# Layer 0 of a two-layer transformer: queries and gates of a head by seven half-size products, key blocks through memory, residual input loaded late

## The reference

```
qkv = silu(x @ qkv_w.T)                 # per head: q, k, v of 128
for blk in blocks:                      # per head
    scores = (q @ k.T) * diag_decay
    out = scores @ v + (q * q_decay) @ kv
    kv = kv * block_decay + (k * k_decay).T @ v
attn = out * rsqrt(mean(out**2) + eps) * norm_w
gate = sigmoid(x @ gate_w.T)
y = (gate * attn) @ out_w.T
x = layernorm(x + y)
```

## Time and profile before

| | |
|---|---|
| median of 3 runs | 3100.72 us |
| profiled execution, own time | 3099.54 us |
| its span | 3097.8 us |
| PE busy | 2976.4 us, 96% |
| DVE, ACT, POOL busy | 63%, 48%, 51% |
| mean granted clock of PE | 0.986 of full speed |
| end of layer 0's attention | about 1160 us |

### The profile page before, as it was taken

One profiled execution on the slowest core, in us unless ns is written; L12 is line 12 of the kernel. 1 busy time (PEld: TensorE's weight loads), 2 busy tenths in 40 slices (PEclk: granted clock), 3 DMA queues, 4 the chain that ended last, 5 costly groups with the idle time before them and its releaser, 6 DMA issues. The chain is left out here.

```text
span 3097.8 us, 56941 instructions
## 1 busy us (share of the span) xinstructions
PE 2976.4 (96%) x17632; PEld 2666.8 (86%) x17632; DVE 1946.6 (63%) x3061; ACT 1490.4 (48%) x2887; POOL 1574.9 (51%) x1075
## 2 busy tenths in 40 slices
PE   7999999999999987799999999999999999996998
PEld 7999999999999976799898998989998989885886
DVE  3445454454545456577777777777777777775565
ACT  3333333333333322466666666666666666663221
POOL 3333333333333331366666666566666666654664
PEclk9999999999999998899999999999999999998999
DMA  4211221121211110366666666656666666655541
GB/s 126 60 51 57 59 61 51 52 62 56 59 51 54 56 28 25 100 206 196 204 205 193 205 196 203 209 189 205 204 199 201 197 202 206 196 195 180 152 142 48
DMA packets 311499, 413.83 MB, mean 134 GB/s; under 512 B 35968, under 2 KB 242832, under 8 KB 311312
## 3 DMA queue, kind: packets, MB, share of 16 engines
q1 hardware_dynamic: 273728, 278.05, 31.2%
q10 hardware_dynamic: 37680, 135.02, 11.0%
q0 software_dynamic: 32, 0.02, 0.0%
HBM read 259.85 MB, written 136.31 MB: 128 GB/s over the span
## 5 line engine op out<-in xcount | busy, mean ns | idle before, releaser
L1365 ACT ACTIVATE b_prob<-b_s_ps,b_shift 128x1024 f32<-128x1024 f32 x256 | 285.8, 1117 | 347.5 <-DVE b_shift L1515 339.8
L82 PE MATMUL b_pj_kq<-b_w_hi,xT_hi 128*128 128x384 f32 x1008 | 351.7, 349 | 21.6 <-DVE b_nat L1491 20.1
L506 ACT ACTIVATE a_sig<-a_pj 128x512 f32<-128x512 f32 x192 | 114.8, 598 | 486.6 <-PE a_pj L84 486.5
L83 PE MATMUL b_pj_kq<-b_w_lo,xT_hi 128*128 128x384 f32 x1008 | 342.7, 340 | 0.0
L84 PE MATMUL b_pj_kq<-b_w_hi,xT_lo 128*128 128x384 f32 x1008 | 342.6, 340 | 0.0
L1521 DVE STREAM_TRANSPOSE b_blocks<-b_prob 128x1024 f32<-128x1024 f32 x256 | 317.4, 1240 | 25.5 <-ACT b_prob L1365 24.9
L1287 POOL TENSOR_TENSOR b_pT_lo<-b_pT_lo,b_pT_hi 128x1024 fp32r<-128x1024 f32 x128 | 305.0, 2405 | 14.4 <-ACT b_pT_hi L1354 14.3
L1287 POOL TENSOR_TENSOR pT_lo<-pT_lo,pT_hi 128x1024 fp32r<-128x1024 f32 x128 | 305.0, 2405 | 14.1 <-ACT pT_hi L1354 14.1
L1515 DVE TENSOR_REDUCE b_shift<-b_s_ps 128x1 f32<-128x1024 f32 x256 | 307.1, 1200 | 2.4 <-PE b_s_ps L84 2.4
L82 PE MATMUL a_pj<-b_w_hi,xT_hi 128*128 128x256 f32 x1024 | 295.6, 289 | 11.9 <-DVE xT_lo L647 11.3
L401 POOL TENSOR_TENSOR b_w_lo<-b_w_raw,b_w_hi 128x512 fp32r<-128x512 f32 x96 | 123.7, 1289 | 332.3 <-ACT b_w_hi L457 325.4
(11 more groups left out here) (257 smaller groups left out, 8907.3 us busy)
## 6 DMA issues: line engine op xcount, KB each, us to landing
bounce<-b_blocks ACTq DMA_DIRECT2D x256, 512.0 KB, 3.4
pT_lo<-bounce SPq DMA_DIRECT2D x512, 128.0 KB, 3.1
b_pT_lo<-bounce SPq DMA_DIRECT2D x512, 128.0 KB, 2.8
b_w_raw<-in_w SPq DMA_DIRECT2D x32, 768.0 KB, 5.0
b_w_raw<-in_w SPq DMA_DIRECT2D x95, 256.0 KB, 3.2
a_k_raw<-a_k_blocks SPq DMA_DIRECT2D x512, 32.0 KB, 1.8
a_w_raw<-in_w SPq DMA_DIRECT2D x32, 256.0 KB, 2.7
a_ow_raw<-in_ow SPq DMA_DIRECT2D x32, 256.0 KB, 3.1
```

The costliest lines, as they stand in the source:

```text
L82: pe.matmul(out, w_hi, x_hi, start=first, stop=False)
L83: pe.matmul(out, w_hi, x_lo, start=False, stop=False)
L506: act.activation(out, pj[half][:, :], ACT.Sigmoid).then_inc(sig, 1)
L1365: act.activation(prob[t % 2][:, :], s_ps[t % 2][:, :], ACT.Exp, bias=shift[:, t:t + 1], accum_out=row_sum[:, t:t + 1]).then_inc(exp_done, 1)
```

## The change

Call the gate and query weights of a head the rows of a 2x2 block matrix, with the lower and upper 256 features as its columns: a11, a12 (gate) and a21, a22 (query). The tokens are b11, b12 (lower features, first and second 512 tokens) and b21, b22 (upper). The four results are the gates and queries of either half of the tokens. Before, they take eight products of half the features; now they take seven, P1 to P7, in the form of Strassen's method with fewer additions:

The diff, cut to its core:

```diff
 def move_k(g):
     sp.wait_ge(k_blocked, g + 1)
+    sp.dma_start(k_bounce[...], k_blocks[...]).then_inc(k_moved, 16)
+    sp.wait_ge(k_moved, MOVED * g + 16)
     for c in range(GROUPS):
-        for r in range(GROUPS):
-            sp.dma_start(k_raw[c * BLK:(c + 1) * BLK, r]..., k_blocks[r * BLK:(r + 1) * BLK, c]...)
+        sp.dma_start(k_raw[c * BLK:(c + 1) * BLK]..., k_bounce[:, :, c, :]...)
...
+def weight_sums(g):                                   # POOL, slot 0
+    pool.wait_ge(w_in[Q_W], 32 * (g + 1))
+    wait(pool, proj, NP * g)
+    pool.tensor_tensor(to[S1], raw(a21), raw(a22), ALU.add).then_inc(w_summed, 1)
+    pool.tensor_tensor(to[S3], raw(a11), raw(a21), ALU.subtract).then_inc(w_summed, 1)
+    pool.wait_ge(w_summed, 4 * g + S1)
+    pool.tensor_tensor(to[S2], to[S1], raw(a11), ALU.subtract).then_inc(w_summed, 1)
+    pool.wait_ge(w_summed, 4 * g + S2)
+    pool.tensor_tensor(to[S4], raw(a12), to[S2], ALU.subtract).then_inc(w_summed, 1)
...
+def product(g, p):                                    # PE
+    if p == P1: pe.wait_ge(silu, 6 * g + 3)
+    if p == P6: wait(pe, combined, NC * (g - 1) + C21)
+    if p == P5: wait(pe, combined, NC * (g - 1) + C12)
+    if p == P2: pe.wait_ge(kept, g + 1)
+    if p == P7: pe.wait_ge(combined, NC * g + U2)
+    if p == P4: pe.wait_ge(combined, NC * g + U3)
+    if p == P3: pe.wait_ge(combined, NC * g + C22)
...
+    for k in range(2):
+        last = three_pass(pe, out[:, :], weights[0][:, k, :], weights[1][:, k, :], tokens[0][:, k, :],
+                          tokens[1][:, k, :], first and k == 0, k == 1, True)
...
+def combine(g, bg, n):                                # DVE
+    dve.wait_ge(proj, NP * g + {U2: P6, U3: P7, C22: P5, C21: P4, C12: P3}[n])
+    dve.tensor_tensor(to, onto, c_ps[n in (C22, C12)][:, :], ALU.add).then_inc(combined, 1)
...
-for h in range(2):                                    # SP, start
-    for t in range(4):
-        if h or t not in (K_W, V_W):
-            load_weights(h, t)
+load_weights(0, Q_W)
+load_weights(0, GATE_W)
+sp.dma_start(norm_sb[:, :], norm_w).then_inc(const_in, 16)
 load_decays(0, 0)
-sp.dma_start(sh.x_nat[:, :, :], x.rearrange("(t p) d -> p t d", p=P)).then_inc(x_nat_in, 16)
+for t in range(4):
+    load_weights(1, t)
...
+sp.wait_ge(proj, NP * HEADS)                          # SP, end
+sp.dma_start(sh.x_nat[:, :, :], x.rearrange("(t p) d -> p t d", p=P)).then_inc(const_in, 16)
```

More of the change, by code:

```diff
@@ L252, in l0_attention @@
         state = sb("state", [P, NT, HD])
+        state_flat = state[:, :, :].rearrange("p c d -> p (c d)")
         gated = sb("gated", [P, TOK])
@@ L410, in half_out, with token_sums_low @@
+            def token_sums_low():
+                for n in (2, 3):
+                    pool.wait_ge(x_hi_done, 2 * KB + n + 1)
+                    pool.tensor_tensor(t_lo[n], t_raw[n], f(t_hi[n]), ALU.subtract).then_inc(t_split, 1)
+                pool.wait_ge(x_summed, 2 * KB)
+                pool.memset(sq_sum[:, :], 0.0).then_inc(zeroed, 1)
+                pool.wait_ge(zeroed, 6)
             def half_out(h, b, j):
@@ L496, in sigmoid, with token_sums_high @@
+            def token_sums_high(*which):
+                for n in which:
+                    act.wait_ge(x_summed, 2 * n + 2)
+                    act.activation(t_hi[n], t_raw[n], ACT.Copy).then_inc(x_hi_done, 1)
             def sigmoid(g, bg, s):
-                act.wait_ge(proj, NG * g + s + 1)
+                act.wait_ge(proj, NP * g + s + 1)
                 half = s % 2
-                if s >= GATE.start:
-                    wait(act, gated_done, 2 * (g - 1))
-                    out = gate_T[bg][:, half * HALF:(half + 1) * HALF]
-                else:
-                    wait(act, silu, 6 * g + s - 1 if s >= 2 else 6 * (g - 1) + 5 + s)
-                    out = sig_tmp[half][:, :]
@@ L506, in sigmoid, with keep_first, gate_sigmoid @@
-                act.activation(out, pj[half][:, :], ACT.Sigmoid).then_inc(sig, 1)
+                wait(act, silu, 6 * g + s - 1 if s >= 2 else 6 * (g - 1) + 6 - s)
+                act.activation(sig_tmp[half][:, :], pj[half][:, :], ACT.Sigmoid).then_inc(sig, 1)
+            def keep_first(g, bg):
+                act.wait_ge(proj, NP * g + P1)
+                wait(act, attn, 2 * (g - 1))
+                act.activation(q_T[bg][:, 0:HALF], pj[0][:, :], ACT.Copy).then_inc(kept, 1)
+            def gate_sigmoid(g, bg, half):
+                cut = slice(half * HALF, (half + 1) * HALF)
+                wait(act, gated_done, 2 * (g - 1))
+                if half == 0:
+                    act.wait_ge(proj, NP * g + P2)
+                    act.activation(gate_T[bg][:, cut], pj[0][:, :], ACT.Sigmoid).then_inc(sig, 1)
+                else:
+                    act.wait_ge(combined, NC * g + C12)
+                    act.activation(gate_T[bg][:, cut], gate_T[bg][:, cut], ACT.Sigmoid).then_inc(sig, 1)
@@ L508, in step, with query_sigmoid @@
+            def query_sigmoid(g, bg, half):
+                act.wait_ge(combined, NC * g + (C21, C22)[half])
+                wait(act, silu, 6 * g + 3 + half)
+                act.activation(sig_tmp[half][:, :], q_T[bg][:, half * HALF:(half + 1) * HALF],
+                               ACT.Sigmoid).then_inc(sig, 1)
             def step(h, b, attention, project, output, split):
@@ new lines, in project_group, with weights_of @@
+                for u in range(2):
+                    cut = slice((2 * s + u) * P, (2 * s + u + 1) * P)
+                    for k in range(KB):
+                        last = three_pass(pe, pj[half][:, u * 2 * HD:(u + 1) * 2 * HD], sh.xT_hi[:, k, cut],
+                                          sh.xT_lo[:, k, cut], kv_hi[:, k, :], kv_lo[:, k, :], k == 0,
+                                          k == KB - 1)
+                last.then_inc(proj, 1)
+            def weights_of(at):
+                return w_hi[at[0]][:, at[1], :], w_lo[at[0]][:, at[1], :]
@@ L622, in step @@
                             outputs(h, b, s // 6)
-                    if project:
+                    if project and s < KV.stop:
                         project_group(h + 1, s)
+                    if project and s >= KV.stop:
+                        for p in PRODUCTS[s]:
+                            product(h + 1, p)
                     if output:
@@ L723, in step @@
                             gate_out(h, b, s // 6)
-                    if project and s < GATE.start:
+                    if project and s < KV.stop:
                         silu_half(h + 1, 1 - b, s)
@@ L727, in step @@
                         block_k(h + 1, 1 - b)
+                        combine(h + 1, 1 - b, U2)
+                    if project and s == 6:
+                        combine(h + 1, 1 - b, U3)
+                        combine(h + 1, 1 - b, C22)
+                    if project and s == 7:
+                        query_silu(h + 1, 1 - b, 1)
+                        combine(h + 1, 1 - b, C21)
+                        combine(h + 1, 1 - b, C12)
+                        query_silu(h + 1, 1 - b, 0)
+                    if isinstance(h, int) and h == -1 and s in (1, 2):
+                        token_sum_low(2 - s)
                     if output:
```

231 lines of the change are left out of this document (175 added, 56 removed).

## The result

| | median us | runs | from | to |
|---|---|---|---|---|
| before | 3100.22 | 4 | 3098.2 | 3102.39 |
| changed | 3057.53 | 4 | 3054.36 | 3058.93 |

The ratio is 0.986, with a 95% interval of 0.9846 to 0.9873: 42.7 us less (39 to 48 by the interval). The profiled execution of the changed kernel took 3054.36 us, its span is 3052.4; it is the fastest of the four.

What follows compares the result with a forecast made beforehand. PE was taken to bound the kernel, busy throughout nearly all of layer 0. From 3099.5: -43.4 steady state, +6.0 start, -4.0 tail gives 3058.1; the median being 1.2 higher, 3059 us, range 3052 to 3078.

Steps and rivals of the forecast that it cites:

- Steady state: 31 heads whose projection runs beside another head's attention: 1.40 us less each, 43.4 us in all.
- The six at 0.233: Gate and query projection: 42 matmuls instead of 48 per head, each removed one priced at 0.233 us, 1.40 per head.
- The hand-overs: Sums passed to PE's products and scores in each head: ready in time, cost 0, slacks 1.4 (U3) and 2.8 us (S2).
- The rival of waiting products: Late products in each head wait for DVE's sums: 31 times the mean wait, 3081 at 0.7 us; 8 in 100.
- The start: Up to the first scores: a longer chain brings them near 50 instead of 44.3, +6 us, bounds 0.5 and 9.
- The fall of the clock in PE's first gap: Start, after PE sits some 3.6 us: granted clock assumed 0.50 (1.2 GHz), costing 2.3 us.
- The tail: Last head's scores and the stage behind: 1.7 us from shorter waits plus 2.3 from the clock, -4.0 together.
- X+4.7 for 4.8: Last head's scores, counted from the end of a gate group as ACT sees it: forecast 4.8 us behind, gain 1.7.
- The 2.3 us put on the clock: Stage behind the last head's scores: if the clock holds, up to 4.4 us more come back; 2.3 taken.
- the forecast's own range: Whole kernel: 3052 (start 0.5, tail 6.1, 0.5 of luck) to 3066 us, before widening for small waits.
- The Trainium skill's 131 ns: Each removed 512-column matmul saves only 0.131 us, so 24.4 us instead of 43.4, time 3078; 3 in 100.
- The SBUF turns: POOL's sums stretched to 2.26 us each by sharing SBUF with DVE: PE waits 2.9 per head, time 3149; 4 in 100.

Runs made afterwards that it cites:

- The additions in their way: Changed kernel plus 448-column additions: four on POOL ahead of the weight sums, 3081.36 us; on DVE ahead of U3, four 3140.48 us, two 3091.57 us.
- the kernel with two additions: Changed kernel with two more 448-column additions on DVE ahead of U3 in every head: 3091.57 us.
- two other profiles of the same start: Changed kernel profiled again, 3058.76 us; changed kernel with expert-weight splits moved later in the last step of the attention loop, 3055.23 us.
- the direct-keys kernel: Changed kernel with key blocks sent in 16 direct DMAs again, as before the change: 3067.59 us, ratio to before 0.9897.
- the kernel before with only the keys' way: Kernel before, with only the key blocks sent through memory (one DMA out, four in): 3093.30 us, ratio 0.9974.
- the doubled product: Changed kernel with the first product's six matmuls issued twice in every head: 3103.89 us, ratio to before 1.001.
- the experiments on DVE: Changed kernel with four, then two, more 448-column additions on DVE ahead of U3 in every head: 3140.48 us and 3091.57 us.
- an edit ahead of that queue: Changed kernel with DVE's third and fourth token sums behind the first two silus instead of ahead of them: 3058.60 us.

## Why the prediction was right

3059 was forecast, 3057.5 measured, and the cause is the one named: six matmuls fewer per head in a stream that nothing else held up. That the number hits within 1.5 us is partly luck. Up to the next stage the change is worth 46.5 us in its first profile and 44.4 in its second, against 41.4 forecast; the two lose 1.1 and 7.2 us behind that, in a part that the change leaves alone. The errors of the three terms cancel only in part.

- *Steady state, -43.4 against -47.8.* The six at 0.233 are right: adding six back costs 0.235 each. What I left out is the second head's wait for its keys, 1.5 us that stood in my own rows, which sits in this stage and which the keys' way takes away. The two kernels with one part each show more: in this stage the keys' way is worth 2.4 to 2.8 us, and the products alone 45.0 (1078.09 - 1033.07). That leaves 1.6 us, 0.05 per head; by the distance of the heads (34.94 and 33.47) it is 0.07. A part is that product 7 and the tiles beside it run at 0.230 instead of 0.233 (nine matmuls from 635.90 to 637.97), 0.03 per head; the rest stays open.
- *The hand-overs.* The slacks of 1.4 us behind U3 and of 2.8 behind S2 were read from an order that had no trace yet. The additions in their way measured 1.46 and 2.9. The rival of waiting products was thus 1.46 us away in every head, and the kernel with two additions shows its price: 33.47 to 34.46 us per head.
- *The start, +6 against +3.15* (about +5 in two other profiles of the same start: 49.19 and 49.48). Here errors of several us stand against each other. I took ACT's sigmoid at 25.50 for the third; it is the fourth, the third stands at 22.63 in the kernel before. With 3.1 of wait and 2.3 of slow clock I put the changed one near 31; it is at 24.74. I then left out the time of the splits of S3 and S4 themselves, 3.4 us to 28.14, and charged K and V one turn given to DVE, which did not come. So K and V were done at 36.35 and not 40.5, and the way from there took 11.1 us for 9.6. The fall of the clock in PE's first gap, which I had assumed, is absent in the first profile (1.00 behind 2.26 us of idleness) but there in the second (0.85 behind 3.21), which is most of the way from +3.15 to +5. The first scores' own cold stretch, which I had left as it was, differs between the two by 1.4 us.
- *The tail, -4.0 against -1.85.* The part that follows from waits is right: X+4.7 for 4.8, and the direct-keys kernel gets its 2.33 us wait for a weight back. The 2.3 us put on the clock did not come in the first profile, where it stayed down (0.64 over 12 us); the second has 2.8 in all, the kernel before with only the keys' way has 4.75. The bounds of 1.7 and 6.1 held all of them; a single value could not. (The outer ends of the forecast's own range add up to 3051.7 and 3064.6 from its terms, where it says 3052 and 3066; nothing hangs on it.)
- *The Trainium skill's 131 ns* was given 3 in 100, and the doubled product rules it out here.
- *The SBUF turns* were given 4 in 100 as a danger to POOL's sums. They didn't reach them (0.73 per sum), but the experiments on DVE show that the danger is real in slot 6, where two additions of 0.61 took 3.18. The Trainium skill, "SBUF — State Buffer", section "SBUF: two separate sides", says that a VectorE operation with two SBUF inputs and a GpSimd operation that reads SBUF shut each other out for the whole of whichever starts first. The traces agree. U3 and C22 read PSUM and SBUF and take 1.41 together (604.00) beside POOL's sq_sum of 1.27 (604.37), so they are not held up.

## What to carry to other kernels

When PE is busy without a gap, price a removed matmul at the start-to-start distance of its neighbours in the trace, and then spend the effort on the two ends of the loop: here they were 2.9 and 2.1 us off, of terms of 6 and 4, and the loop 4.4 of 43. Read a slack as the distance between the producer's start and the consumer's place in its queue: up to it a delay costs nothing (1.46 us here), beyond it one for one, and a long stop can cost the clock on top. At the start of a kernel ask which queue the first result passes last; an edit ahead of that queue was worth nothing here until the queue's order was changed. And profile a kernel twice before explaining a microsecond or two of its start: two executions of this one differ by 3.1 us up to the last product.
